# DLRM tower on one Trainium2 core: interleaved subtraction, one-hots and picks, unrolled middle tiles, and an eleventh field picked by matmuls

## What is computed

```
e = jnp.stack([tbl_0[ids[:, 0]], ..., tbl_25[ids[:, 25]]], axis=1)      # 512 x 26 x 128
combined = jnp.concatenate([e, r_dense_x[:, None, :]], axis=1)          # 512 x 27 x 128
interact = jnp.einsum('bfd,bgd->bfg', combined, combined)
z = interact[:, triu_i, triu_j]                                         # 512 x 351
h = jnp.concatenate([z, r_dense_x], axis=1)                             # 512 x 479
h = jnp.maximum(h @ W_top1 + b_top1, 0.0)                               # 512 x 512
h = jnp.maximum(h @ W_top2 + b_top2, 0.0)                               # 512 x 256
y = h @ W_top3                                                          # 512 x 1
```

## Time and profile before

| | |
|---|---|
| median of 3 runs | 109.2 us |
| the profiled execution, its own time | 109.18 us |
| its span, first to last instruction | 107.4 us |
| granted TensorE clock, mean | 0.999 |
| busy share: TensorE, VectorE, ScalarE, GpSimd | 92%, 74%, 70%, 62% |

### The profile page before, as it was taken

The page is one execution under the profiler, slowest core; times in us unless marked ns, Lnnn a source line. Parts: engine busy times, 40 slices in busy tenths (PEclk is TensorE's granted clock), DMA queues, the critical chain, the costliest instruction groups (busy, mean ns, idle before and its releaser), DMA issues.

```text
span 107.4 us, 2605 instructions
## 1 busy us (share of the span) xinstructions
PE 98.5 (92%) x998; PEld 79.0 (74%) x998; DVE 79.8 (74%) x162; ACT 75.0 (70%) x149; POOL 66.3 (62%) x72
## 2 busy tenths in 40 slices
PE   5999899989799999999798978999999989998992
PEld 1356676657467675887478958999999979997991
DVE  6599999999999999999943974588338922685120
ACT  4499999999999999999706842475527732474430
POOL 3777777777777787777877777777777750000000
PEclk9999999999999999999999999999999999999999
DMA  3852749995663636621211221221121220000000
GB/s 46 334 209 58 235 76 372 374 345 113 217 197 101 221 78 218 225 92 49 55 49 49 53 50 49 63 66 49 49 55 49 58 67 3 6 0 0 6 0 1
DMA packets 5200, 11.64 MB, mean 108 GB/s; under 512 B 1979, under 2 KB 2491, under 8 KB 5189
## 3 DMA queue, kind: packets, MB, share of 16 engines
q1 hardware_dynamic: 3120, 7.27, 21.2%
q0 software_dynamic: 2048, 4.20, 14.2%
q10 hardware_dynamic: 20, 0.02, 0.1%
HBM read 11.48 MB, written 0.00 MB: 107 GB/s over the span
## 4 chain that ended last, share of the span: by engine, by line
DVE 46%; PE 44%; issue 6%; ACT 2%; POOL 0%; DVEq 0%; POOLq 0%
DVE onehot L464 22%; PE gram_ps L613 13%; DVE low L476 13%; PE top_ps L678 5%; PE tr_ps L594 5%; PE act_ps L667 4%; PE dve_ps L667 4%; DVE onehot L470 3%; DVE xt L473 2%; PE gram_ps L578 2%; PE top_ps L702 2%; PE tr_ps L653 1%; DVE xt L450 1%; PE dve_ps L626 1%; PE act_ps L626 1%
## 5 line engine op out<-in xcount | busy, mean ns | idle before, releaser
L287 POOL DMA_INDIRECT rows<-table,ids_sb x64 | 65.5, 1023 | 20.8 <-issue 19.2
L578 PE MATMUL gram_ps<-onehot,high 128*128 128x512 f32 x82 | 23.1, 410 | 1.9 <-DVE onehot L464 1.6
L578 PE MATMUL gram_ps<-onehot,low 128*128 128x512 f32 x82 | 22.1, 411 | 0.0
L578 PEld LDWEIGHTS gram_ps<-onehot,high 128*128 128x128 f32 x82 | 14.3, 188 | 8.8 <-DVE onehot L464 5.0
L578 PEld LDWEIGHTS gram_ps<-onehot,low 128*128 128x128 f32 x82 | 15.4, 189 | 3.9
L464 DVE TENSOR_TENSOR onehot<-dve_ps,row_f 128x1024 fp32r<-128x1024 f32 (+1 forms) x10 | 14.4, 1479 | 1.2 <-PE act_ps L554 1.2
L464 DVE TENSOR_TENSOR onehot<-gram_ps,row_f 128x1536 fp32r<-128x1536 f32 (+1 forms) x10 | 14.9, 1531 | 0.0
L613 PE MATMUL gram_ps<-xt 128*58 128x52 f32 x512 | 14.5, 217 | 0.3 <-issue 0.3
L483 DVE COPY gram_sb<-gram_ps 26x208 f32<-26x208 f32 x32 | 12.0, 376 | 3.6 <-PE gram_ps L613 2.4
L613 PEld LDWEIGHTS gram_ps<-xt 128*58 128x58 f32 x512 | 14.0, 133 | 0.9 <-issue 0.5
L385 ACT ACTIVATE onehot<-onehot 128x1344 fp32r<-128x1344 f32 (+1 forms) x10 | 14.3, 1426 | 0.0
(11 more groups left out here) (83 smaller groups left out, 111.7 us busy)
## 6 DMA issues: line engine op xcount, KB each, us to landing
table<-table SPq DMA_DIRECT2D x9, 512.0 KB, 3.6
rows<-table,ids_sb POOLq DMA_INDIRECT x64, 2.9
w1p_sb<-w_pairs SPq DMA_DIRECT2D x1, 768.0 KB
table<-table SPq DMA_DIRECT2D x1, 640.0 KB, 3.8
w_sb<-w SPq DMA_DIRECT2D x1, 512.0 KB
dense_sb<-dense SPq DMA_DIRECT2D x1, 256.0 KB, 5.1
w1d_sb<-w_dense SPq DMA_DIRECT2D x1, 256.0 KB
ids_sb<-ids SPq DMA_DIRECT2D x1, 52.0 KB, 2.0
```

The costliest lines, as they stand in the source:

```text
L287: pool.indirect_dma_start(rows[:, t, s - 1, :], None, tables[f], bass.IndirectOffsetOnAxis(ids_sb[:, t, f:f + 1], 0)).then_inc(gathered[t] ...
L578: last = pe.matmul(pick_ps[b][:], weights[:, c, :], onehot[:, b, c, :], start=(c == 0 and part == 0), stop=(c == CHUNKS[o] - 1 and part == 1))
```

## The change

- `ONEHOT` gets an eleventh field, number 2, with 1250 rows (ten chunks). Fifteen fields are gathered for each tile: 60 indirect DMAs.
- VectorE makes whole chunks of one-hots, one instruction for each (six or five chunks in turn, seven for the two large tables); ScalarE makes the rest (two or three).
- VectorE's order: a piece of the subtraction of field `o`, a one-hot chunk of field `o + 1`, in turn. TensorE's order: a piece of `low` of field `o`, then one `high` chunk of field `o + 1`, in turn.
- Only a small selection matrix is made before the first spread; the other selections are made after it. The padding of `xt` is cleared by three engines near the start.
- The banks of transposes are 4, 4, 4 and 3 wide (4, 4, 4, 2, 1 for the last tile), those of tiles 0 and 1 stand in or right behind the first stage. `gram(1)` follows `gram(0)` after half of `dense_part(0)`. The hardware loops are written out. In the last tile `dense_part(3)` and `back_last` stand between the two halves of `second_layer(2)`.

```diff
-ONEHOT = [0, 4, 7, 11, 12, 13, 15, 17, 23, 1]
-FIELD_ROWS = [1000] * 9 + [1250]
+ONEHOT = [0, 4, 7, 11, 12, 13, 15, 17, 23, 1, 2]
+FIELD_ROWS = [1000] * 9 + [1250] * 2
-DVE_CHUNKS = {8: ((0, 1), (2, 3, 4)), 10: ((0, 1, 2), (3, 4, 5))}
-SHARED_COLS = {8: 192, 10: 368}
+DVE_CHUNKS = [6 if o % 2 == 0 else 5 for o in range(NO - 2)] + [7, 7]
...
             def onehots(o):
-                part = onehot[:, o % 2].rearrange("k c b -> k (c b)")[:, CHUNKS[o] * B - act_cols(o):CHUNKS[o] * B]
+                part = onehot[:, o % 2, DVE_CHUNKS[o]:CHUNKS[o]]
                 act.wait_ge(ids_spread, o + 1)
                 if o >= 2:
                     act.wait_ge(pick_done, o - 1)
-                for c in range(shared(o), CHUNKS[o]):
-                    at, cols = act_part(o, c)
-                    last = act.activation(part[:, at:at + B - cols], ids_ps_act[o % 2][:, cols:], ACT.Abs,
-                                          bias=row_neg[:, c:c + 1])
+                for c in range(DVE_CHUNKS[o], CHUNKS[o]):
+                    last = act.activation(onehot[:, o % 2, c], ids_ps_act[o % 2], ACT.Abs, bias=row_neg[:, c:c + 1])
...
+            dve.wait_ge(ids_spread, 1)
+            onehots(0, range(DVE_CHUNKS[0]))
             for o in range(NO):
                 dve.wait_ge(high_ready, o + 1)
-                for c in rest_pieces(o):
-                    dve.tensor_tensor(low[:, b, c], table[:, o % TABLES, c], high[:, b, c].bitcast(F32),
-                                      ALU.subtract).then_inc(low_ready, 1)
+                if o + 1 < NO:
+                    dve.wait_ge(ids_spread, o + 2)
+                for r, piece in enumerate(rest_pieces(o)):
+                    rest(o, piece)
+                    if o + 1 < NO:
+                        if r == 0 and o >= 1:
+                            dve.wait_ge(pick_done, o)
+                        onehots(o + 1, (r,))
+                if o + 1 < NO:
+                    onehots(o + 1, range(REST, DVE_CHUNKS[o + 1]))
...
+            def pick_high(o, chunks):
+                b = o % 2
+                for c in chunks:
+                    if c == 0:
+                        if o >= 2:
+                            pe.wait_ge(pick_out, o - 1)
+                        pe.wait_ge(high_ready, o + 1)
+                    if c < DVE_CHUNKS[o]:
+                        pe.wait_ge(onehot_dve, DVE_BEFORE[o] + c + 1)
+                    elif c == DVE_CHUNKS[o]:
+                        pe.wait_ge(onehot_act, o + 1)
+                    pe.matmul(pick_ps[b][:], high[:, b, c, :], onehot[:, b, c, :], start=(c == 0), stop=False,
+                              skip_group_check=True)
...
-            for o in range(NO - 1):
-                pick(o, 0)
+            pick_high(0, range(CHUNKS[0]))
+            for o in range(NO):
                 if o + 2 < NO:
                     spread(o + 2)
-                pick(o, 1)
+                for r in range(REST):
+                    pick_low(o, r)
+                    if o + 1 < NO:
+                        pick_high(o + 1, (r,))
+                if o + 1 < NO:
+                    pick_high(o + 1, range(REST, CHUNKS[o + 1]))
...
+                if o == NO - 2:
+                    transposes(1, (0, 1))
+            transposes(1, (2, 3))
             pe.wait_ge(pad_zero, TILES)
             pe.wait_ge(pick_out, NO)
             gram(0)
+            pe.wait_ge(weights_in, WEIGHTS)
+            dense_part(0, (0, 1))
+            gram(1)
+            transposes(2, (0, 1))
+            back(0)
+            dense_part(0, (2, 3))
+            first_layer(0, range(N1 // P))
...
+            gram(3)
+            dense_part(3, (0, 2, 1, 3))
+            second_layer(2, (0,))
+            back_last(2)
+            second_layer(2, (1,))
+            back_last(1)
+            back_last(0)
```

322 lines of the change are left out of this document (161 added, 161 removed).

## The result

The changed kernel takes **134.51 us** (median of 4 runs, 133.45 to 135.16); the kernel before took 109.19 us beside it. The ratio is 1.231, 95% interval 1.225 to 1.237: slower. The profiled execution took 134.51 us with a span of 132.6 us, so 1.9 us lie around the span. The forecast was 125.8 us and its range ended at 129.5.

The account below looks back on a forecast made before the run. VectorE and ScalarE bound the first stage; the change makes a ring pace each field. gram(0) at 76.5 us, plus 36.2 second stage, 9.4 end, 1.9 rest and 1.8 around the span: 125.8 us, range 121.5 to 129.5.

Parts of the forecast that it names:

- the time until field 0 is picked: First stage, start: VectorE's one-hots and subtractions of field 0, then two matmuls, done at 12.6 us.
- the waits of the second stage: Second stage: 2.4 us of waits assumed, with none and 3.1 us as the ends.
- What bounds the kernel now: Kernel before: VectorE and ScalarE bound the first stage at about 4.5 us a field, TensorE the second.
- The ring: First stage, each field: ScalarE's copy, Abs and high, then TensorE's matmuls, wait in a circle; 5.6 or 6.15 us in turn.
- VectorE alone: First stage: VectorE by itself needs 0.60 us per one-hot chunk and 4.6 us a field on average.
- The first one-hot starts at 5.15: Start of the kernel: ids converted by 3.20 us, two selections 1.96 us, then VectorE's first one-hot at 5.15 us.
- Rival 3, the clock: TensorE's clock falls to half rate after waits in the first stage: 1.6 us more for each ring; chance 6%.
- a fall in each ring: Clock rival's full case: half-rate matmuls in every turn of the first stage, eight intervals costing 1.6 us more; 141 us.
- The second stage: From gram(0) to the end of gram(3): 30.5 us work, 3.3 us transposes, 2.4 us waits; 36.2 us, to 112.7.
- The end: From the last gram to the last copy: 9.4 us instead of 9.89, half of second_layer(2) filling a 0.50 us wait.
- The rest of the span adds 1.9 us: After the last copy to the end of the span: 1.9 us, taken from the kernel before (107.4 - 105.54).
- The three upward bounds: Range above the forecast: 2.5 us for ten rings, 0.7 us for second-stage waits, 2 us for one fall of the clock.

## Why the forecast missed

The sign, the place and the mechanism were right; the size was 8.7 us too small, and the range did not hold it. The steps that failed are terms of the sum: the falls of the clock, left out of it (4.5 us measured); the time until field 0 is picked, 12.6 us (15.5 measured); the transfer of `y` inside the 1.9 us of the rest (3.3 measured); and the waits of the second stage, 0.9 us too low. By the steps of the prediction:

- *What bounds the kernel now:* held. Wherever the ring was opened, VectorE and ScalarE filled the stage again and a field took 4.5 us on average.
- *The ring:* held to 0.15 us in nearly every field. 5.52 to 5.55 and 6.09 us were measured where the clock stood, against 5.6 and 6.15; field 8 took 6.34 (6.4), field 9 7.45 (7.6), field 10 4.77 (4.9); with fillers, field 1 took 6.16 (6.4) and field 2 8.21 (8.3). All lie below the forecast, 1.0 us in sum, and so hid a part of the other misses. Both ways to open it gave 15 us back, the falls included.
- *"VectorE alone":* held. Two one-hots started at 41.18 and what stands behind them at 42.38, 0.60 us each. The Trainium skill's 125 ns for each VectorE instruction on PSUM (Perfetto Trace Analysis, Optimizing Scalar/DVE Operations) would make it 0.66 us, by estimate; the 67 ns of the trace held.
- *"The first one-hot starts at 5.15":* failed, 2.6 us. Two terms. The selections were scaled by their columns, 0.98 us each, and took 1.65 and 1.67; a tenth more columns nearly doubled the time, and the row for ten blocks did not carry over to eleven. And the padding moved to GpSimd was costed at nothing at the start without a reason (a cover is named only behind field 0): it runs from 1.40 to 2.80 us beside VectorE's conversion, and holds it for 1.35 us. The conversion reaches the end in full, the selections by some 0.4 us. A third of field 0's 2.9 us is neither: its last `low` matmuls stand behind field 1's first `high`, with ScalarE, the second spread and the warm-up matmuls ahead of it. The prediction saw this ring from field 1 on, and forgot it in field 0.
- *Rival 3, the clock:* its mechanism came true beside the ring. The price of a fall held (1.6 us; 1.3 to 1.6 measured), their number did not. The text knew two cases: a fall in each ring (141 us, 6%) or a single one, "2 us, inside my range". What happened lies between, three falls for 4.5 us, and the argument against it ("the trace has no fall at its waits") rested on a trace whose waits were short: once it works, TensorE waits 0.93 us at the longest, ahead of a transpose at 53.90 (0.50 us in the earlier trace rows). With waits of 1 to 3 us the trace of before could not speak for either side, and the case of a few falls should have been in the range and in the likeliest sum.
- *"The second stage":* 0.9 us too low. It took 37.1 us; the 3.1 us of waits before, which were one of the two ends, would have been the better value. TensorE's work fell by ten transposes, 1.1 us by the prediction's own price, and the stage by 0.8 us: the new order did not shorten the waits, and with the old first stage it did not either. Which wait kept them was not isolated.
- *"The end":* 9.3 us against 9.4, held.
- *"The rest of the span adds 1.9 us":* failed, 3.3. It was copied from before as if fixed, but it contains the transfer of `y`, and that is 1.0 to 1.5 us longer in every eleven-field kernel. Why it is stays open.

The range left 3.7 us above the forecast. The three upward bounds that the prediction names (2.5, 0.7 and 2 us) add up to 5.2, and even 131.0 would not have held 134.5. The falls alone, 4.5 us, pass the 3.7; the start (2.9) and `y` (1.4) point the same way, and for these the range had nothing.

## What to carry to other kernels

Before interleaving two streams on an in-order engine, follow each new wait back through the orders of the other engines until it comes round to itself: if it does, the sum around the ring is the new period, and here it could be read from the old trace to 0.1 us in the plain fields. Interleaving was harmless once the producer of the first waiting operand ran one round ahead. Apply the same to the first field, where other work may stand in the ring. When a ring opens gaps of over a microsecond on TensorE, as it did here in eight fields, add some falls of the clock as a likely cost, not as a remote rival. A stage that became shorter may only have handed work to its neighbour, so compare between two points that both kernels reach alike; and when an engine gets faster or its work shifts in time, look at what else was hidden by a hair, here GpSimd's issues, which turned a gain of 1.8 us into nothing.

## What the runs showed of the hardware

- The granted clock of TensorE fell to the lower level for 3.4 us at a time, three times in the changed kernel, soon after waits of 1.4 to 3.3 us; each fall cost 1.3 to 1.6 us. With the same waits filled by zero matmuls, the filled fields had none. Waits of 1.68, 1.82 and (in a ten-field version) 2.48 us were not followed by a fall, and executions of one kernel differ in the number of falls.
- A conversion of 128x10 numbers on VectorE took 1.59 us beside GpSimd's two memsets and 0.24 without them. In the other direction, GpSimd's issue of an indirect DMA grew from 0.94 to 1.66 or 1.76 us where it met VectorE's subtractions of two SBUF operands; behind a memset it grew by 0.08 us only.
- A comparison on VectorE with ten blocks of 128 columns took 0.86 to 0.89 us on 10, 32 or 128 partitions, one with eleven blocks 1.65 to 1.67 us on 11, 32 or 128.
- The same 2 KB of output landed after 1.42 us in the six kernels with ten picked fields and after 2.4 to 2.95 us in the eight with eleven, with nothing else on its queue.
